# Expert feed-forward on 71 token tiles: first matmul with its weights as the loaded operand, second in high and low parts

## The chip, the cores and the metric

The kernel runs on one core of a Trainium2 chip, in one launch. TensorE (PE, with its weight loads shown as PEld), VectorE (DVE), ScalarE (ACT), GpSimd (POOL) and the DMA queues of SyncE and GpSimd run side by side and wait for each other on semaphores. The metric is the device time of one execution in microseconds.

## The reference

`x` is 16 sequences of 256 rows with 512 columns (4096 rows), and the program applies four blocks to it, each as `x = x + tanh(gate) * block(layernorm(x))`. The change is in the last, a mixture of 8 experts with the best 2 for each row:

```python
router_logits = x_flat @ w_router
top_vals, top_idx = jax.lax.top_k(router_logits, TOP_K)          # 2 of 8
probs = jax.nn.softmax(top_vals, axis=-1)
w_tok = jnp.zeros((N, E)).at[rows, top_idx].add(probs)
h = jnp.einsum('nc,ecd->ned', x_flat, w_fc)                      # 512 -> 512
h = jnp.square(jax.nn.relu(h))
y = jnp.einsum('ned,edc->nec', h, w_proj)                        # 512 -> 512
out = jnp.einsum('nec,ne->nc', y, w_tok)
```

The blocks before it (a long convolution mixed with per-head products, a gated sum over 32 small experts, a cross attention with 8 heads) are the same in both kernels.

## The kernel before

After attention the kernel computes the router's logits, picks two experts for each row, counts, and lays the 8192 (row, expert) picks out in tiles of 128 picks that all belong to one expert: `TILES9` = 71 tiles. `slots` holds for each tile the row number of each of its 128 picks, `share` the weight of each, and `TEi` for each tile the offset of its expert in the weights. `WF` and `WP` keep all eight experts' first and second weights in SBUF, 8 x 2048 float32 per partition each.

The stage for the experts, from about 1187 us to the end, works tile by tile:

- `gather(j)` (POOL): an indirect DMA brings the 128 normed rows of the tile from DRAM into `xs[j % 3]`.
- `across(j)` (PE, L1511): four float32 transposes turn the rows into `pX`; `columns(j)` (DVE, L1823) copies them to `xc[j % 2]`.
- `up(j)` (PE, L1519): four float32 matmuls, with 128 columns of `xc` as the loaded operand and 512 columns of the expert's `WF` moving. A float32 matmul shows as two records, so eight records. The result has picks on the partitions.
- ReLU (ACT, L1654) into `hr`; `back(j)` (PE, L1526): four float32 transposes; the square (ACT, L1657) into `hT`.
- `down(j)` (PE, L1534): four float32 matmuls, `hT` loaded, `WP` moving, into `pY`.
- scaling by `share` (DVE, L1832) into `ys[j % 2]`, and a scatter (POOL, L1336), an indirect DMA that adds the rows to the output in DRAM. Each scatter waits until the one before has landed (`s_add9`).

Each engine has its instructions in the order in which they are written, and waits where a semaphore asks it to. `after(signal, eng, n)` waits only for n above 0; the buffers of this stage are double, and a producer waits by it for the consumer of two tiles ago. PE's order is `up(j + 1)`, `across(j + 2)`, `down(j)`, `back(j + 1)` for each j. The small buffers of this stage lie in `XN`, which until then held the rows of x.

## Time and profile before

| | us |
|---|---|
| median of 3 runs | 1759.55 (1759.21 to 1763.59) |
| the profiled execution | 1759.9 |
| its span, first to last instruction | 1758.2 |
| PE busy | 1593.6 (91%) |
| DVE busy | 931.6 (53%) |
| ACT busy | 710.3 (40%) |
| POOL busy | 960.2 (55%) |

Busy time is read per engine, and an average over stages with different limits says little of one stage; in the views that follow the stage of the experts is cut out. A merged row of a timeline stands for several instructions ("x8"), with the start of the first and the time to the end of the last. Matmuls are pipelined, so the spacing of their starts, not the duration of one, is what a run of them costs. "L1519" is line 1519 of the kernel.

### The profile page before, as it was taken

The numbers are of one execution on the slowest core, as the hardware profiler recorded it, in microseconds if no ns is written. First come the engines' busy times: TensorE is split into PE (matmuls) and PEld (weight loads), VectorE is DVE, ScalarE is ACT, GpSimd is POOL, SyncE is SP. The second block draws the span as 40 slices with busy tenths as digits, with TensorE's granted clock in tenths as the row PEclk, the third lists the DMA queues.
The fourth block names the chain that finished last, engine by engine and source line by source line (L and its number), as shares of the span: only waits on it lengthen the run. The fifth ranks groups of instructions, "written<-read, shape, count | busy, mean of one in ns | idle before, by whom it ended". The sixth has DMA issues, their size and how long they took to land.

```text
span 1758.2 us, 24233 instructions
## 1 busy us (share of the span) xinstructions
PE 1593.6 (91%) x6970; PEld 881.5 (50%) x6970; DVE 931.6 (53%) x1555; ACT 710.3 (40%) x1367; POOL 960.2 (55%) x978
## 2 busy tenths in 40 slices
PE   5999999987584499999999999868999999999997
PEld 4677777765251244444444443564444444444443
DVE  7788888887365467777777774361111111111111
ACT  6332333226327167777777777531111111111111
POOL 4788888864027367888888888202333333333332
PEclk9999999988697589999999999969999999999999
DMA  6344434438358945666666661832334334334333
GB/s 237 126 131 140 138 131 131 135 114 216 61 174 287 240 109 140 163 162 162 156 157 151 155 157 38 293 138 60 64 69 72 65 68 72 65 67 72 66 66 48
DMA packets 110375, 224.00 MB, mean 127 GB/s; under 512 B 12257, under 2 KB 12257, under 8 KB 109409
## 3 DMA queue, kind: packets, MB, share of 16 engines
q1 hardware_dynamic: 94400, 185.88, 37.0%
q0 software_dynamic: 15904, 37.23, 12.1%
q8 instruction: 38, 0.62, 0.1%
q14 instruction: 33, 0.26, 0.1%
HBM read 146.71 MB, written 75.84 MB: 127 GB/s over the span
## 4 chain that ended last, share of the span: by engine, by line
PE 62%; DVE 1%; ACT 1%; DMA 1%; issue 0%; SPq 0%; POOL 0%; DVEq 0%; ACTq 0%; POOLq 0%
PE pA L1519 14%; PE pO L1534 14%; PE pB L1370 9%; PE pO L1380 7%; PE pA L1352 7%; PE pO L1393 4%; PE pA L1511 2%; PE pB L1526 2%; PE pO L1503 1%; PE pB L1361 1%; PE pA L1442 1%; PE pA L1449 1%; DVE low L1668 0%; PE pB L1468 0%; DMA qs<-q_low 0%
## 5 line engine op out<-in xcount | busy, mean ns | idle before, releaser
L1668 DVE TENSOR_REDUCE low<-pA 128x2 f32<-128x1024 f32 x256 | 307.7, 1223 | 145.9 <-PE pA L1352 134.8
L1599 ACT ACTIVATE pt<-pB 128x512 f32<-128x512 f32 x512 | 287.1, 593 | 128.6 <-PE pB L1370 123.2
L424 PE MATMUL y<-kv,toep 128*128 128x288 f32 x1280 | 327.8, 413 | 9.0 <-DVEq L63 5.8
L1336 POOL DMA_INDIRECT out_rows<-XN,slots x71 | 112.6, 1587 | 357.5 <-DVE XN L1832 353.4
L424 PEld LDWEIGHTS y<-kv,toep 128*128 128x128 f32 x1280 | 239.0, 191 | 97.5 <-DVEq L63 34.0
L1519 PE MATMUL pA<-WF,XN 128*128 x568 | 257.8, 597 | 1.1 <-DVE XN L1823 0.9
L1534 PE MATMUL pO<-WP,XN 128*128 x568 | 255.6, 593 | 0.8 <-ACT XN L1657 0.8
L1370 PE MATMUL pB<-qs,ks 98*128 98x512 f32 x512 | 229.3, 452 | 2.7 <-ACT pt L1599 2.4
L1352 PE MATMUL pA<-ks,qs 96*128 96x512 f32 x512 | 190.7, 418 | 34.4 <-DMA qs<-q_low 33.0
L1370 PEld LDWEIGHTS pB<-qs,ks 98*128 98x128 f32 x512 | 97.0, 191 | 192.5 <-ACT pt L1599 150.2
L1823 DVE COPY XN<-pA 128x512 f32<-128x512 f32 x71 | 49.1, 691 | 258.3 <-PE pA L1511 258.3
L1304 POOL TENSOR_TENSOR part_sum<-pt 128x1024 f32<-128x1024 f32 x64 | 152.1, 2377 | 20.3 <-ACT pt L1599 12.9
L1832 DVE TENSOR_SCALAR XN<-pO,share 128x512 f32<-128x512 f32 x71 | 53.3, 751 | 200.2 <-PE pO L1534 200.2
L1309 POOL TENSOR_TENSOR part_sum<-part_sum,pt 128x1024 f32<-128x1024 f32 x64 | 152.4, 2381 | 7.0 <-POOL part_sum L1304 3.8
L1519 PEld LDWEIGHTS pA<-WF,XN 128*128 128x128 f32 x568 | 103.2, 192 | 104.8 <-issue 104.8
L1534 PEld LDWEIGHTS pO<-WP,XN 128*128 128x128 f32 x568 | 102.5, 190 | 103.3 <-issue 103.3
L1657 ACT ACTIVATE XN<-pB 128x512 f32<-128x512 f32 x71 | 42.4, 597 | 260.2 <-PE pB L1526 260.2
L394 ACT ACTIVATE ym<-y 128x384 f32<-128x384 f32 (+1 forms) x128 | 52.5, 410 | 230.7 <-PE y L424 230.7
L1380 PE MATMUL pO<-pt,vt 128*32 128x512 f32 x1024 | 136.6, 607 | 0.0
L1352 PEld LDWEIGHTS pA<-ks,qs 96*128 96x128 f32 x512 | 100.9, 200 | 61.0 <-DMA qs<-q_low 34.5
L1654 ACT ACTIVATE XN<-pA 128x512 f32<-128x512 f32 x71 | 42.4, 597 | 216.0 <-PE pA L1519 216.0
L362 POOL TENSOR_TENSOR R<-ym,qc 128x384 f32<-128x384 f32 (+1 forms) x128 | 99.2, 795 | 55.8 <-ACT ym L394 54.7
(252 smaller groups left out, 2006.8 us busy)
## 6 DMA issues: line engine op xcount, KB each, us to landing
ks<-ctx_high SPq DMA_DIRECT2D x64, 256.0 KB, 4.7
qs<-q_high SPq DMA_DIRECT2D x64, 256.0 KB, 6.3
kc<-in_ctx_conv SPq DMA_DIRECT2D x32, 384.0 KB, 5.4
XN<-in_x SPq DMA_DIRECT2D x16, 512.0 KB, 10.0
toep<-kernel_and_skip SPq DMA_DIRECT2D x32, 256.0 KB, 3.5
ct<-in_ctx SPq DMA_DIRECT2D x16, 512.0 KB, 6.4
ctx_high<-kh SPq DMA_DIRECT2D x16, 512.0 KB, 4.4
ctx_low<-kl SPq DMA_DIRECT2D x16, 512.0 KB, 5.1
```

The source lines that it names most:

```text
L362: pool.tensor_tensor(ap(R[half], n0 * 4 * HD0 + 1, [[4 * HD0, n], [HD0 + 1, D4 - 1], [1, HD0]]), ap(ym[half], n0 * MID, [[MID, n], [HD0, D ...
L424: m = pe.matmul(y[half].rearrange("p (l n) c -> p l n c", l=CB)[:, l, :, 0:PAIRS], toep[u][:, (l - s) * P:(l - s + 1) * P], kv[u][:, half, ...
L1304: pool.tensor_tensor(part_sum[:, 2 * n:2 * n + 2], pt[0][:, 2 * n:2 * n + 2], pt[1][:, 2 * n:2 * n + 2], ALU.add).then_inc(s_add, 1)
L1309: pool.tensor_tensor(part_sum[:, 2 * n:2 * n + 2], part_sum[:, 2 * n:2 * n + 2], pt[2][:, 2 * n:2 * n + 2], ALU.add).then_inc(s_add, 1)
L1336: pool.indirect_dma_start(out=out["out"], out_offset=bass.IndirectOffsetOnAxis(ap=slots[:, j:j + 1], axis=0), in_=ys[j % 2], in_offset=Non ...
L1352: m = pe.matmul(pA[n % 2][:, half, :], qs[u][0:NS, h, m0:m0 + P].bitcast(F32R), ks[u][0:NS, h, :].bitcast(F32R), start=True, stop=True)
L1370: pe.matmul(bank(u, n), ks[u][0:NS + 2, h, s * P:(s + 1) * P].bitcast(F32R), qs[u][0:NS + 2, h, :].bitcast(F32R), start=True, stop=True).t ...
L1380: m = pe.matmul(pO[u % 2][h * HD1:(h + 1) * HD1, :], vt[u][:, s, h * HD1:(h + 1) * HD1], pt[s][:, h, :], start=(s == 0), stop=(s == CB - 1))
L1519: m = pe.matmul(pH[j % 2], xc[j % 2][:, k, :], ap(WF, e + k * C, [[1, C]]), start=(k == 0), stop=(k == CB - 1))
L1534: m = pe.matmul(pY[j % 2], hT[j % 2][:, k, :], ap(WP, e + k * C, [[1, C]]), start=(k == 0), stop=(k == CB - 1))
L1599: act.activation(pt[s][:, h, :], bank(u, n), ACT.Exp, scale=SCALE1).then_inc(s_exp, 1)
L1668: dve.tensor_reduce(ap(low[u % 2], t % CB * NH + t // CB, [[NH, 2], [1, 1]]), pA[n % 2], op=ALU.max, axis=AX.X, negate=True).then_inc(s_re ...
```

## The change

The first matmul's operands trade places: the expert's weights are loaded, 128 x 128 at a time, and the tile's 128 columns move. So `pH` holds the hidden values with the hidden dimension on the partitions (block b in columns 128b to 128b + 127), and `back` is not needed. ACT copies the tile's expert weights out of `WF` into `fc[j % 2]` first (`fc_at`), 2048 float32 per partition.

The second matmul is done in float32r, as three products: high part of the hidden values by high part of the weights, high by low, and low by high. ACT makes the weights' high part by a copy that rounds to float32r (`proj_high`), DVE the low part as the difference (`proj_low`, one buffer only). For the hidden values ACT takes the ReLU into `hq` (`picks_above`), DVE multiplies it with max(pH, 0) to have the square (`squares`), ACT rounds it to `hh` (`picks_high`), and DVE takes the difference into `hl` (`picks_low`). The new buffers lie where `XN` lies.

```diff
--- before.py
+++ after.py
@@ -97,6 +97,11 @@
     s_eps = sem("s_eps")
     s_gates = sem("s_gates")
 
+    with ExitStack() as rows:
+        sb(rows, "tiles", [P, 8 * C])
+        hh, hl = ([sb(rows, f"{n}{i}", [P, C]) for i in range(2)] for n in ("hh", "hl"))
+        fc, wph = ([sb(rows, f"{n}{i}", [P, CB * C]) for i in range(2)] for n in ("fc", "proj_high"))
+        wpl = sb(rows, "proj_low", [P, CB * C])
     XN = sb(whole, "XN", [P, UNITS, ROW])
 
     def x_rows(b):
@@ -1087,14 +1092,13 @@
             sem(n + "_7", st) for n in ("s_t", "s_ev", "s_l", "s_lg", "s_m", "s_gap", "s_e2", "s_took", "s_pos",
                                         "s_in", "s_R", "s_w", "s_dve", "s_cnt", "s_Q", "s_V", "s_W", "s_pl", "s_wz", "s_slots")]
 
-        xc, hr, hT, ys = ([ap(XN, (3 + 2 * n + i) * C, [[1, C]]) for i in range(2)] for n in range(4))
-        xc, hT = ([t.rearrange("p (k n) -> p k n", n=P) for t in ring] for ring in (xc, hT))
+        xc, ys = ([ap(XN, (3 + 2 * n + i) * C, [[1, C]]) for i in range(2)] for n in range(2))
+        hq = ap(XN, 7 * C, [[1, C]])
         pX, pH = ([bank[:, i] for i in range(2)] for bank in pA)
         pX = [bank.rearrange("p (k n) -> p k n", n=P) for bank in pX]
-        pG = [bank.rearrange("p (k n) -> p k n", n=P) for bank in pB]
         pY = pO
-        s_xt, s_xc, s_h, s_hr, s_g, s_hT, s_y, s_ys, s_add9 = [sem(n + "_9", st) for n in (
-            "s_xt", "s_xc", "s_h", "s_hr", "s_g", "s_hT", "s_y", "s_ys", "s_add")]
+        s_xt, s_xc, s_h, s_hr, s_hq, s_low, s_w9, s_y, s_ys, s_add9 = [sem(n + "_9", st) for n in (
+            "s_xt", "s_xc", "s_h", "s_hr", "s_hq", "s_low", "s_w", "s_y", "s_ys", "s_add")]
 
         def after(signal, eng, n):
 
@@ -1512,43 +1516,35 @@
                 t.then_inc(s_xt, 1)
 
             def up(j):
-                e = pe.value_load(TEi[0:1, j:j + 1], min_val=0, max_val=(E1 - 1) * CB * C)
+                pe.wait_ge(s_w9, 2 * j + 1)
                 pe.wait_ge(s_xc, j + 1)
-                after(s_hr, pe, j - 1)
-                for k in range(CB):
-                    m = pe.matmul(pH[j % 2], xc[j % 2][:, k, :], ap(WF, e + k * C, [[1, C]]), start=(k == 0), stop=(k == CB - 1))
+                after(s_hq, pe, j - 1)
+                for b in range(CB):
+                    for k in range(CB):
+                        m = pe.matmul(pH[j % 2][:, b * P:(b + 1) * P], fc[j % 2][:, k * C + b * P:k * C + b * P + P], xc[j % 2][:, k * P:(k + 1) * P],
+                                      start=(k == 0), stop=(k == CB - 1))
                 m.then_inc(s_h, 1)
 
-            def back(j):
-                pe.wait_ge(s_hr, j + 1)
-                after(s_hT, pe, j - 1)
-                for k in range(CB):
-                    t = pe.transpose(pG[j % 2][:, k, :], hr[j % 2][:, k * P:(k + 1) * P], ident)
-                t.then_inc(s_g, 1)
-
             def down(j):
-                e = pe.value_load(TEi[0:1, j:j + 1], min_val=0, max_val=(E1 - 1) * CB * C)
-                pe.wait_ge(s_hT, j + 1)
+                pe.wait_ge(s_low, 2 * j + 2)
                 after(s_ys, pe, j - 1)
                 for k in range(CB):
-                    m = pe.matmul(pY[j % 2], hT[j % 2][:, k, :], ap(WP, e + k * C, [[1, C]]), start=(k == 0), stop=(k == CB - 1))
+                    rows = slice(k * P, (k + 1) * P)
+                    weights = slice(k * C, (k + 1) * C)
+                    for n, (picks, proj) in enumerate(((hh, wph[j % 2]), (hh, wpl), (hl, wph[j % 2]))):
+                        m = pe.matmul(pY[j % 2], picks[j % 2][:, rows].bitcast(F32R), proj[:, weights].bitcast(F32R),
+                                      start=(k == 0 and n == 0), stop=(k == CB - 1 and n == 2))
                 m.then_inc(s_y, 1)
 
             across(0)
-            pe.wait_ge(s_wf, 16 * E1)
             up(0)
             across(1)
-            back(0)
-            pe.wait_ge(s_wp, 16 * E1)
-            pe.wait_ge(s_slots, 2)
             for j in range(TILES9):
                 if j + 1 < TILES9:
                     up(j + 1)
                 if j + 2 < TILES9:
                     across(j + 2)
                 down(j)
-                if j + 1 < TILES9:
-                    back(j + 1)
...
@@ -1648,13 +1644,42 @@
                                        scale=ap(weight, c * G + n, [[1, 1]]))
                 m.then_inc(s_W, 1)
 
+            def fc_at(j):
+                e = act.value_load(TEi[0:1, j:j + 1], min_val=0, max_val=(E1 - 1) * CB * C)
+                after(s_h, act, j - 1)
+                act.activation(fc[j % 2], ap(WF, e, [[1, CB * C]]), ACT.Copy).then_inc(s_w9, 1)
+
+            def proj_high(j):
+                e = act.value_load(TEi[0:1, j:j + 1], min_val=0, max_val=(E1 - 1) * CB * C)
+                after(s_y, act, j - 1)
+                act.activation(wph[j % 2].bitcast(F32R), ap(WP, e, [[1, CB * C]]), ACT.Copy).then_inc(s_w9, 1)
+
+            def picks_above(j):
+                act.wait_ge(s_h, j + 1)
+                after(s_low, act, 2 * j - 1)
+                act.activation(hq, pH[j % 2], ACT.Relu).then_inc(s_hr, 1)
+
+            def picks_high(j):
+                act.wait_ge(s_hq, j + 1)
+                after(s_y, act, j - 1)
+                act.activation(hh[j % 2].bitcast(F32R), hq, ACT.Copy).then_inc(s_hr, 1)
+
+            act.wait_ge(s_slots, 1)
+            act.wait_ge(s_wf, 16 * E1)
+            fc_at(0)
+            act.wait_ge(s_wp, 16 * E1)
+            proj_high(0)
+            fc_at(1)
+            picks_above(0)
+            picks_high(0)
             for j in range(TILES9):
-                act.wait_ge(s_h, j + 1)
-                after(s_g, act, j - 1)
-                act.activation(hr[j % 2], pH[j % 2], ACT.Relu).then_inc(s_hr, 1)
-                act.wait_ge(s_g, j + 1)
-                after(s_y, act, j - 1)
-                act.activation(hT[j % 2], pG[j % 2], ACT.Square).then_inc(s_hT, 1)
+                if j + 1 < TILES9:
+                    proj_high(j + 1)
+                if j + 2 < TILES9:
+                    fc_at(j + 2)
+                if j + 1 < TILES9:
+                    picks_above(j + 1)
+                    picks_high(j + 1)
 
         @block.vector
         def _(dve):
@@ -1820,16 +1845,43 @@
             def columns(j):
                 dve.wait_ge(s_xt, j + 1)
                 after(s_h, dve, j - 1)
-                dve.tensor_copy(xc[j % 2], pX[j % 2]).then_inc(s_xc, 1)
-
-            columns(0)
-            columns(1)
-            for j in range(TILES9):
-                if j + 2 < TILES9:
-                    columns(j + 2)
+                dve.tensor_copy(xc[j % 2], pX[j % 2].rearrange("p k n -> p (k n)")).then_inc(s_xc, 1)
+
+            def proj_low(j):
+                e = dve.value_load(TEi[0:1, j:j + 1], min_val=0, max_val=(E1 - 1) * CB * C)
+                dve.wait_ge(s_w9, 2 * j + 2)
+                after(s_y, dve, j)
+                dve.tensor_tensor(wpl.bitcast(F32R), ap(WP, e, [[1, CB * C]]), wph[j % 2], ALU.subtract).then_inc(s_low, 1)
+
+            def squares(j):
+                dve.wait_ge(s_h, j + 1)
+                dve.wait_ge(s_hr, 2 * j + 1)
+                dve.scalar_tensor_tensor(hq, pH[j % 2], 0.0, hq, ALU.max, ALU.mult).then_inc(s_hq, 1)
+
+            def picks_low(j):
+                dve.wait_ge(s_hr, 2 * j + 2)
+                dve.tensor_tensor(hl[j % 2].bitcast(F32R), hq, hh[j % 2], ALU.subtract).then_inc(s_low, 1)
+
+            def scaled(j):
                 dve.wait_ge(s_y, j + 1)
                 after(s_add9, dve, 16 * (j - 1))
                 dve.tensor_scalar(ys[j % 2], pY[j % 2], share[:, j:j + 1], None, ALU.mult).then_inc(s_ys, 1)
+
+            columns(0)
+            columns(1)
+            squares(0)
+            picks_low(0)
+            for j in range(TILES9):
+                if j > 0:
+                    scaled(j - 1)
+                proj_low(j)
+                if j + 1 < TILES9:
+                    squares(j + 1)
+                if j + 2 < TILES9:
+                    columns(j + 2)
+                if j + 1 < TILES9:
+                    picks_low(j + 1)
+            scaled(TILES9 - 1)
 
 
 # ---- launch: one core; numpy lays the inputs out, and takes the output's rows apart again ----
```

On PE the place is the middle of the stage, one tile. Names: `pA` holds `pX` and `pH`, `pB` is `pG`, `pO` is `pY`, `XN` are the small buffers, `s_x90` the landing of a gather. Before:

```order
L1519 MATMUL pA<-WF,XN 128x512
L1511 MATMUL pA<-ident,XN 128x128 [waits s_xc_9,s_x90]
L1511 MATMUL pA<-ident,XN 128x128 x3
L1530 TENSOR_LOAD TEi
L1530 ISA x2
L1534 ISA [waits s_ys_9,s_hT_9]
L1534 MATMUL pO<-WP,XN 128x512
```

and with the change:

```order
L1524 MATMUL pA<-XN,fc 128x128 [waits s_hq_9,s_xc_9,s_w_9]
L1524 MATMUL pA<-XN,fc 128x128 x15
L1515 MATMUL pA<-ident,XN 128x128 [waits s_xc_9,s_x90]
L1515 MATMUL pA<-ident,XN 128x128 x3
L1535 MATMUL pO<-proj_high,hh 128x512 [waits s_ys_9,s_low_9]
L1535 MATMUL pO<-proj_low,hh 128x512
L1535 MATMUL pO<-proj_high,hl 128x512
```

`across` keeps its place between `up` and `down`; the transposes of L1526 are gone, the loads of the expert's offset too, and `down` now waits for the low parts.

On DVE, one tile in the same place. Before:

```order
L1832 TENSOR_SCALAR XN<-pO,share 128x512 [waits s_add_9,s_y_9]
L1823 COPY XN<-pA 128x512 [waits s_h_9,s_xt_9]
L1832 TENSOR_SCALAR XN<-pO,share 128x512 [waits s_add_9,s_y_9]
L1823 COPY XN<-pA 128x512 [waits s_h_9,s_xt_9]
L1832 TENSOR_SCALAR XN<-pO,share 128x512 [waits s_add_9,s_y_9]
```

and with the change:

```order
L1868 TENSOR_SCALAR XN<-pO,share 128x512 [waits s_add_9,s_y_9]
L1851 TENSOR_LOAD TEi
L1851 ISA x2
L1854 ISA [waits s_y_9,s_w_9]
L1854 TENSOR_TENSOR proj_low<-WP,proj_high 128x2048
L1859 SCALAR_TENSOR_TENSOR XN<-pA,XN 128x512 [waits s_hr_9,s_h_9]
L1848 COPY XN<-pA 128x512 [waits s_h_9,s_xt_9]
L1863 TENSOR_TENSOR hl<-XN,hh 128x512 [waits s_hr_9]
L1868 TENSOR_SCALAR XN<-pO,share 128x512 [waits s_add_9,s_y_9]
```

The scaling (L1868) now has `proj_low` right behind it, and `squares`, `columns` and `picks_low` stand between that and the next scaling.

On ACT, one tile. Before there are only the ReLU (L1654) and the square (L1657):

```order
L1654 ACTIVATE XN<-pA 128x512 [waits s_g_9,s_h_9]
L1657 ACTIVATE XN<-pB 128x512 [waits s_y_9,s_g_9]
L1654 ACTIVATE XN<-pA 128x512 [waits s_g_9,s_h_9]
L1657 ACTIVATE XN<-pB 128x512 [waits s_y_9,s_g_9]
L1654 ACTIVATE XN<-pA 128x512 [waits s_g_9,s_h_9]
```

and with the change:

```order
L1653 TENSOR_LOAD TEi
L1653 ISA x2
L1655 ISA [waits s_y_9]
L1655 ACTIVATE proj_high<-WP 128x2048
L1648 TENSOR_LOAD TEi
L1648 ISA x2
L1650 ISA [waits s_h_9]
L1650 ACTIVATE fc<-WF 128x2048
L1660 ACTIVATE XN<-pA 128x512 [waits s_low_9,s_h_9]
L1665 ACTIVATE hh<-XN 128x512 [waits s_y_9,s_hq_9]
```

The two long copies stand ahead of the ReLU of the next tile.

## Rows read from the trace of the kernel before

**Rows 1.** The page: busy us by engine; the chain that ended last, by line.

```profile
PE 1593.6 (91%) x6970; PEld 881.5 (50%) x6970; DVE 931.6 (53%) x1555; ACT 710.3 (40%) x1367; POOL 960.2 (55%) x978
...
PE pA L1519 14%; PE pO L1534 14%; PE pB L1370 9%; PE pO L1380 7%; PE pA L1352 7%; PE pO L1393 4%; PE pA L1511 2%; PE pB L1526 2%; PE pO L1503 1%; PE pB L1361 1%; PE pA L1442 1%; PE pA L1449 1%; DVE low L1668 0%; PE pB L1468 0%; DMA qs<-q_low 0%
```

**Rows 2.** Chain of waits in order of time: start us, us, engine, line.

```profile
1193.14 5.77 PE pA L1519 x8
...
1204.59 3.44 PE pO L1534 x8
1208.47 3.44 PE pA L1519 x8
...
1735.12 3.44 PE pA L1519 x8
...
1743.06 4.84 DMA out_rows<-XN,slots
1748.67 1.55 POOL out_rows L1336
```

**Rows 3.** Busy us of PE, PEld, DVE, ACT, POOL; granted clock; 1200 to 1740.

```profile
1200.00:1740.00 540.00, 539.78 (x1671) 266.02 (x1669) 99.57 (x139) 83.58 (x140) 175.73 (x136) 1.00 0.38 67
```

**Rows 4.** Timeline of one tile: start us, us, engine, line, op.

```profile
1351.58 3.60 PE L1534 MATMUL pO<-WP,XN 128*128 x8
...
1355.02 0.60 PE L1526 MATMUL pB<-ident,XN 128*128 128x128 f32 x4
...
1355.22 0.75 DVE L1832 TENSOR_SCALAR XN<-pO,share 128x512 f32<-128x512 f32 x1 [2.75 <-PE pO L1534]
...
1355.46 3.60 PE L1519 MATMUL pA<-WF,XN 128*128 x8
...
1356.25 1.59 POOL L1336 DMA_INDIRECT out_rows<-XN,slots  x1 [4.87 <-DVE XN L1832]
```

**Rows 5.** Timeline of PE at full clock, float32 with short moving operands.

```profile
487.80 2.40 PE L785 MATMUL pk<-RB,WV 128*128 128x64 f32 x20
...
1181.83 4.29 PE L1503 MATMUL pO<-XN 128*128 128x142 f32 x34
```

**Rows 6.** Timeline of PE in attention; L1352 and L1370 are float32r.

```profile
701.78 0.39 PE L1352 MATMUL pA<-ks,qs 96*128 96x512 f32 x1
...
702.71 0.42 PE L1370 MATMUL pB<-qs,ks 98*128 98x512 f32 x1
...
704.05 0.50 PE L1370 MATMUL pB<-qs,ks 98*128 98x512 f32 x1
...
704.86 0.39 PE L1352 MATMUL pA<-ks,qs 96*128 96x512 f32 x1
...
705.18 1.07 PE L1380 MATMUL pO<-pt,vt 128*32 128x512 f32 x8
```

**Rows 7.** Groups by line and form (mean ns); L1515, ns min/median/max.

```profile
L968 ACT ACTIVATE WV<-WV 128x1024 fp32r<-128x1024 f32 x16 | 16.9, 1057 | 0.5
...
L913 ACT ACTIVATE room<-WV 128x512 f32<-128x512 f32 x16 | 10.0, 626 | 0.0
L1750 DVE TENSOR_TENSOR XN<-numbers,inside 128x1024 f32<-128x1024 f32 x8 | 9.8, 1221 | 0.4
...
L1772 DVE TENSOR_TENSOR XN<-numbers,tile 128x568 f32<-128x568 f32 x8 | 6.0, 744 | 0.4 <-PE pO L1503 0.3
...
L1515 PEldq TENSOR_LOAD <-TEi x71: 296/301/490, 1191.2 to 1731.5; - x71
```

**Rows 8.** Timelines in which DVE starts while POOL works.

```profile
27.87 1.89 POOL L145 TENSOR_TENSOR kv<-kc 128x1024 f32<-128x1024 f32 x1 [2.42 <-DMA kc<-in_ctx_conv]
27.96 1.83 DVE L222 SCALAR_TENSOR_TENSOR work_<-mv,rstd_ 128x8 f32<-128x8 f32 x1
...
1097.01 4.82 POOL L1309 TENSOR_TENSOR part_sum<-part_sum,pt 128x1024 f32<-128x1024 f32 x2
...
1097.78 1.72 DVE L1782 CAST numbers<-numi 128x161 f32<-128x161 int32 x1
```

## The prediction

> **What bounds the kernel now.** I read the page first: TensorE is busy 91% of the span, and two lines of the expert stage, L1519 and L1534, make 28% of the chain that ended last [rows 1]. Then the chain in order of time [rows 2]: from 1204.59 us to the end of the matmuls it is L1534, L1519, L1534, L1519 without a break, eight records in 3.44 us each, and a pair comes every 7.745 us (1208.47 to 1735.12 is 68 pairs). Then the busy times between 1200 and 1740 us [rows 3]: PE 539.78 of 540 us at full granted clock (1.00, that is 2.4 GHz), DVE 99.57, ACT 83.58, POOL 175.73. So the change is worth what it does to PE's sum per tile, as long as the other three keep up.
>
> The timeline of one tile [rows 4] gives that sum as differences of starts. L1534 at 1351.58 to L1526 at 1355.02 is 3.44 us for eight records, 0.430 each; L1526 at 1355.02 to L1519 at 1355.46 is four transposes, 0.109 each. 16 x 0.430 + 8 x 0.109 = 7.75, the measured 7.745. A merged row outlasts its spacings by the last record's overhang: 3.60 - 3.44 = 0.16.
>
> **PE, part by part.**
> - `up` was 3.44 us. Now it is 16 float32 matmuls, thus 32 records of 128 columns, each with its own weight load. Nearest rows at full clock [rows 5], overhang taken off: L1503, 142 columns and new weights for each record, (4.29 - 0.16)/34 = 0.121, what 142 columns take in proportion to L1519; L785, only 64 columns, (2.40 - 0.16)/20 = 0.112, so there the loads set the pace. The transposes, 128 columns, show 0.109. I take 0.112, 3.58 us; bounds 0.109 (3.49) and 0.121 (3.87).
> - `across` stays, 0.44. `back` goes, -0.44.
> - `down` was 3.44. Now it is 12 float32r records of 512 columns. In attention [rows 6] four such start between 701.78 and 702.71 (three spacings and the merged one counted: 0.93 us for four), 0.233 each: 2.80 us. The other end is half of L1519's 0.430, 0.215: 2.58.
> - Switches between float32 and float32r come twice per tile, new in this stage. The L1370 that follows float32 at 704.05 lasts 0.50 in place of 0.39, +0.11. Leaving, L1352 at 704.86 to L1380 at 705.18 is 0.32 in place of 0.233, +0.09 [rows 6]. Bounds 0 and 0.30 per tile (both, and half as much again); I take 0.15, since PE's look ahead may hide one of them behind `across`.
>
> Sum: 3.58 + 0.44 + 2.80 + 0.15 = 6.97 us in place of 7.745, so -0.775 per tile.
>
> The Trainium skill, "TensorE: Matmul & The Clock Gate", section "Part 3: Packing small matmuls", says that a weight load overlaps matmuls in flight only where their row groups differ; here all use all rows, so by that rule each record would pay its load and its stream in turn. The trace disagrees: L1503 and L1519 run at 0.121 and 0.430 with a full-row load for each record. It is rival 3.
>
> **What must hide beside it.** Durations for 2048 elements are drawn on from two sizes [rows 7]. ACT, SBUF to SBUF: 512 in 0.626, 1024 in 1.057, so 2048 in 1.92 us. DVE with two SBUF inputs: 568 in 0.744, 1024 in 1.221, so 2048 in 2.29 us.
> - ACT per tile: two copies 3.84, ReLU 0.60, float32r copy 0.63: 5.07 us, where it was 83.58 over 69.7 tiles, 1.2. Fits in 6.97.
> - DVE: `columns` 0.69, `scaled` 0.75 [rows 4], `proj_low` 2.29, `squares` 0.75 (as `scaled`, one PSUM input of 512), `picks_low` 0.69: 5.17 us, where it was 1.4. Fits.
> - The expert's number is read from SBUF twice on ACT and once on DVE. On PE that read takes 0.30 us [rows 7] of the sequencer, with two register steps perhaps 0.5, while the engine works. On ACT it comes behind a copy of 0.63 or 1.92, on DVE behind `scaled`: hidden, charged nothing; exposed it is 0.5 on DVE, and 1.0 on ACT.
> - The single `proj_low` buffer is the tightest wait. DVE may write it when `down(j-1)` is over, and `down(j)` waits for it; behind `down(j)` on PE stand `up(j+2)` and all else. Between them PE has `up(j+1)` and `across(j+2)`, 4.02 us. DVE has the handover 0.2 (overhang 0.16 and 0.04: 1355.18 to 1355.22), `scaled` 0.75 and `proj_low` 2.29: 3.24. Cover left: 0.8 us.
> - The long ring spans two tiles: from the end of `down(j-1)` on, `proj_high(j+1)` 1.92, `fc_at(j+2)` 1.92, ReLU 0.60, `squares` 0.75, `columns` 0.69, `picks_low` 0.69, `scaled` 0.75, `proj_low` 2.29, `down(j+1)` 2.80: 12.41, with handovers 13.0, against 13.94. Cover left: 0.9 us per two tiles.
> - POOL's program is the same. Its loop: a scatter lands 4.84 us after its start, and the next starts 0.77 after that (1743.06 + 4.84 = 1747.90, 1748.67) [rows 2]: 5.61 us per tile, under 6.97.
>
> **Start and end.** `up(0)` waits for the same `columns(0)` as now, 1193.14, in a slow stretch (5.77 us for eight records, 3.44 later); `fc_at(0)`, ready with the slots before the first gather, is done by then. `down(0)` waits for `up(0)` (1198.9), `across(1)` and `columns(1)` (1200.1), `squares`, the copy, `picks_low` and `proj_low`: 1204.5, where it is 1204.59 now. The last `down(70)` waits for `scaled` and `proj_low` after `down(69)`, 3.2 us where `back` and the square now take 1.4; it is 0.6 shorter itself, and some of the rest runs beside the scatter chain behind it. Together +0.5 us.
>
> **The sum.** 69 spacings x -0.775 = -53.5, and +0.5: -53. The profiled execution took 1759.9 us (span 1758.2), the median of the three runs is 1759.55. 1759.9 - 53 = 1706.9; against the median it would be 1706.5. I say 1706. This case's own ends: best 3.49 + 0.44 + 2.58 = 6.51, -85, 1675; worst 3.87 + 0.44 + 2.80 + 0.30 = 7.41, -23, 1737.
>
> **Rivals.**
> 1. *The ring through ACT and DVE decides.* For it: ACT goes from 1.2 to 5.1 us per tile and DVE from 1.4 to 5.2, in a ring with 0.9 us of cover per two tiles; exposed reads of the expert's number would use that up. Against: each sum alone fits, and handovers are 0.04. With 2.0 us more the ring is 15.0, 7.5 per tile: 69 x -0.245 = -17, 1743.
> 2. *The port that DVE and POOL share; it ends slower.* DVE's cast of 161 elements takes 1.72 us [rows 8]: it starts inside the first of two POOL additions (1097.01, 2.4 each) and ends at 1099.50, just as that one ends. Another DVE operation, on 8 elements with two SBUF inputs, starts at 27.96 and ends at 29.79, POOL's ends at 29.76. So one holds the other off for a whole instruction. `proj_low` lasts 2.29 us, has two SBUF inputs, and starts right behind `scaled`, which is what wakes the scatter 0.28 later (1355.97, 1356.25 in [rows 4]). If each scatter is held 2.29, its loop is 5.61 + 2.29 = 7.90: 71 x +0.155 = +11, 1771. It decides from a hold of 1.36 per tile (6.97) and loses from 2.13 (7.745). The other way round, `proj_low` held for the scatter's 1.59, makes 3.24 + 1.59 - 4.02 = +0.81, 7.78 per tile, 1762. Against: a scatter that starts late in its tile meets only the rest of `proj_low`, so the hold shrinks before it binds, and DVE starts first by 0.3 us.
> The Trainium skill, "SBUF — State Buffer", section "SBUF: two separate sides", calls the pair an exclusive lock, which a DVE operation with two SBUF inputs takes only against a GpSimd one that reads SBUF. The two rows agree. Whether an indirect DMA's issue is held too, no row shows.
> 3. *Weight loads exposed in `up`.* The loads' pace 0.112 plus half of 0.215 for 128 columns is 0.219, `up` 7.0 us, the tile 10.4: +183, 1943. L1503 speaks against it.
>
> **How the numbers follow.** The forecast has 0.75, rival 1 0.10, rival 2 0.09 (0.07 by the scatter's loop, 0.02 by a held DVE), rival 3 0.02; 0.04 is left for what I don't see. The range 1680 to 1745 cuts the forecast's fast tail, where all bounds fall well at once, and takes in rival 1. What a measurement can tell from no change is 0.3%, about 5 us. Faster by more: 0.75 + 0.10 + 0.01 = 0.86; within: 0.04; slower: 0.10.
>
> **What would show it.** Right: in the stage's chain, 32 records of `up` 0.112 apart, 12 of `down` 0.233 apart with the first some 0.1 longer, pairs every 6.9 to 7.0 us, PE still busy nearly throughout. Wrong: PE idle before `down` with `proj_low` as releaser (its cover is gone), before `up` with `fc` or the columns (rival 1); `scaled` waiting for a landed scatter, or a scatter longer than 1.59 (rival 2); `up` near 0.2 apart (rival 3). My number fails if float32r takes more than 0.233 with 128 rows of weights, or a switch more than 0.15.

## The result, and the profile after

The changed kernel takes 1698.9 us (median of 4 runs, 1694.96 to 1701.35), beside 1759.99 for the kernel before on the same chip (1759.21 to 1763.59): a ratio of 0.9647, interval 0.962 to 0.9673. The forecast was 1706 with a range of 1680 to 1745. The profiled execution took 1696.54 us, its span is 1694.8.

First the page: busy time by engine, then the head of the chain that ended last, by line. They answer to [rows 1].

```profile
PE 1525.5 (90%) x8674; PEld 1054.9 (62%) x8674; DVE 1185.5 (70%) x1768; ACT 969.3 (57%) x1509; POOL 1043.7 (62%) x978
...
DMA out_rows<-XN,slots 22%; PE pB L1374 10%; PE pO L1384 8%; PE pA L1356 7%; PE pO L1397 4%; PE pO L1535 1%; PE pO L1507 1%; PE pA L1524 1%; DMA XN<-normed_rows,slots 1%; PE pB L1365 1%; PE pA L1446 1%; PE pA L1453 1%; DVE low L1693 1%; PE pB L1472 0%; POOL out_rows L1340 0%
```

TensorE is 68 us less busy, DVE 254 and ACT 259 us more. The chain hardly names `up` and `down` any more (L1524 and L1535, 1% each); it names the scatters. That is a trap, and the next view shows it: the busy times of PE, PEld, DVE, ACT and POOL and the granted clock, in the stage's steady part (as [rows 3]) and while the last `down` runs.

```profile
1200.00:1670.00 470.00, 466.94 (x3291) 429.79 (x3290) 345.26 (x345) 331.38 (x276) 254.69 (x135) 1.00 0.43 77
...
1679.00:1684.00 5.00, 5.00 (x12) 3.80 (x12) 0.00 (x0) 0.00 (x0) 1.38 (x1) 0.50 0.41 52
```

PE is still busy 99.3% of the steady part, so PE's sum per tile is still what a tile costs. The chain goes through the scatters because each of them starts 0.81 us after the one before has landed (median of tiles 5 to 65), and the walk back never leaves that loop. What is new is 3 us of idle PE in the first row and a clock of 0.50 in the second.

The timeline of one tile (start us, us, engine, line, operation; rows between are left out at "..."), which answers to [rows 4]:

```profile
1402.60 3.77 PEld L1524 LDWEIGHTS pA<-XN,fc 128*128 128x128 f32 x32
...
1402.82 3.73 PE L1524 MATMUL pA<-XN,fc 128*128 128x128 f32 x32
...
1403.02 0.75 DVE L1868 TENSOR_SCALAR XN<-pO,share 128x512 f32<-128x512 f32 x1 [0.31 <-PE pO L1535]
...
1403.83 2.29 DVE L1854 TENSOR_TENSOR proj_low<-WP,proj_high 128x2048 fp32r<-128x2048 f32 x1
...
1404.94 2.64 POOL L1340 DMA_INDIRECT out_rows<-XN,slots  x1 [2.84 <-DMA out_rows<-XN,slots]
...
1406.39 0.60 PE L1515 MATMUL pA<-ident,XN 128*128 128x128 f32 x4
...
1406.74 0.48 PE L1535 MATMUL pO<-proj_high,hh 128*128 128x512 f32 x1
...
1407.06 0.40 PE L1535 MATMUL pO<-proj_low,hh 128*128 128x512 f32 x1
...
1407.30 0.40 PE L1535 MATMUL pO<-proj_high,hl 128*128 128x512 f32 x1
```

L1524 is `up`: 1402.82 to 1406.39 is 3.57 us for 32 records, 0.1115 each. L1535 is `down`. Its first record shows 0.35 after `across` started, before four transposes of 0.109 can be through, and the second comes 0.32 later to make up for it; after that the records stand 0.24 and 0.23 apart. From the end of `across`'s four spacings (1406.39 + 0.44 = 1406.83) to the next `up` at 1409.60 it is 2.77 us. The usual spacing from `up` to `up` is 3.57 + 0.435 + 2.77 = 6.77 us, where it was 7.745.

The groups by line and form (busy us, mean ns, then idle before and its releaser) show the two things that were new to me: the scatters' issue takes 2.74 us where it took 1.59 [rows 4], and PE waits at `across` for a gather. Of those waits 5.0 us stood in the kernel before too, ahead of its first tiles, as the last row shows; the other 2.8 are new.

```profile
L1340 POOL DMA_INDIRECT out_rows<-XN,slots x71 | 194.7, 2742 | 215.4 <-DMA out_rows<-XN,slots 181.0 <-DVE XN L1868 34.4
...
L1515 PE MATMUL pA<-ident,XN 128*128 128x128 f32 x284 | 43.7, 277 | 7.8 <-DMA XN<-normed_rows,slots 7.7
```

```profile
L1511 PE MATMUL pA<-ident,XN 128*128 128x128 f32 x284 | 43.1, 275 | 5.0 <-DMA XN<-normed_rows,slots 5.0
```

### The profile page after: what moved, and what is told of

Read it like the earlier page. It is cut to its first block, busy times and chain, and to the rows that moved or that the text cites. A ratio compares the mean times of both kernels' runs of the same rounds, so it can differ in the third digit from the quotient of the medians.

```text
span 1694.8 us, 27929 instructions
## 1 busy us (share of the span) xinstructions
PE 1525.5 (90%) x8674; PEld 1054.9 (62%) x8674; DVE 1185.5 (70%) x1768; ACT 969.3 (57%) x1509; POOL 1043.7 (62%) x978
## 4 chain that ended last, share of the span: by engine, by line
PE 35%; DMA 23%; issue 3%; DVE 2%; ACT 1%; POOL 0%; SPq 0%; POOLq 0%; DVEq 0%; ACTq 0%
DMA out_rows<-XN,slots 22%; PE pB L1374 10%; PE pO L1384 8%; PE pA L1356 7%; PE pO L1397 4%; PE pO L1535 1%; PE pO L1507 1%; PE pA L1524 1%; DMA XN<-normed_rows,slots 1%; PE pB L1365 1%; PE pA L1446 1%; PE pA L1453 1%; DVE low L1693 1%; PE pB L1472 0%; POOL out_rows L1340 0%
## 5 line engine op out<-in xcount | busy, mean ns | idle before, releaser
L1340 POOL DMA_INDIRECT out_rows<-XN,slots x71 | 194.7, 2742 | 215.4 <-DMA out_rows<-XN,slots 181.0
L1524 PEld LDWEIGHTS pA<-XN,fc 128*128 128x128 f32 x2272 | 266.1, 193 | 7.7 <-ACT fc L1650 1.2
L1524 PE MATMUL pA<-XN,fc 128*128 128x128 f32 x2272 | 266.8, 276 | 1.7 <-DVE XN L1848 1.7
L1655 ACT ACTIVATE proj_high<-WP 128x2048 fp32r x71 | 135.8, 1912 | 81.1 <-PE pO L1535 81.1
L1854 DVE TENSOR_TENSOR proj_low<-WP,proj_high 128x2048 fp32r<-128x2048 f32 x71 | 162.8, 2293 | 5.6 <-issue 1.6
L1650 ACT ACTIVATE fc<-WF 128x2048 f32 x71 | 134.5, 1894 | 4.7 <-DVEq L1843 4.7
L150 POOL TENSOR_TENSOR kv<-kc 128x1024 f32<-128x1024 f32 x64 | 121.1, 1892 | 5.0 <-PEq L418 3.1
L1029 POOL DMA_INDIRECT XN<-normed_rows,slots x71 | 70.5, 993 | 83.1 <-DVEq L1843 60.8
L1535 PE MATMUL pO<-proj_high,hh 128*128 128x512 f32 x284 | 117.8, 415 | 3.5 <-DVE proj_low L1854 3.5
```

What stands on the lines that cost most here:

```text
L1340: pool.indirect_dma_start(out=out["out"], out_offset=bass.IndirectOffsetOnAxis(ap=slots[:, j:j + 1], axis=0), in_=ys[j % 2], in_offset=Non ...
L1524: m = pe.matmul(pH[j % 2][:, b * P:(b + 1) * P], fc[j % 2][:, k * C + b * P:k * C + b * P + P], xc[j % 2][:, k * P:(k + 1) * P], start=(k ...
L1655: act.activation(wph[j % 2].bitcast(F32R), ap(WP, e, [[1, CB * C]]), ACT.Copy).then_inc(s_w9, 1)
L1854: dve.tensor_tensor(wpl.bitcast(F32R), ap(WP, e, [[1, CB * C]]), wph[j % 2], ALU.subtract).then_inc(s_low, 1)
```

## The experiments

`e1` to `e4` ran on one chip, `e5` to `e8` on another, `e9` to `e11` on a third, each group beside the kernel before, whose median there was 1760.08, 1757.45 and 1758.21 us; so across groups it is the ratios to it that compare. Every edit is shown against the changed kernel, with lines left out at "...". "Spacing" is the median time from one `up` to the next; "excess" is what the 68 spacings from tile 2 to tile 70 take beyond 68 such medians; the tail is from the start of `up(70)` to the end of the span. All three are read from the one profiled execution of each kernel. Before: spacing 7.745, excess 0, tail 23.2. After: 6.773, 4.8, 25.5.

### The two halves of the change alone

`e1`: `up` is turned, its weights are copied by ACT, the squares go straight to `down`, and `down` stays float32 from `WP`.

```diff
-                    for n, (picks, proj) in enumerate(((hh, wph[j % 2]), (hh, wpl), (hl, wph[j % 2]))):
-                        m = pe.matmul(pY[j % 2], picks[j % 2][:, rows].bitcast(F32R), proj[:, weights].bitcast(F32R), ...
+                    m = pe.matmul(pY[j % 2], hh[j % 2][:, k * P:(k + 1) * P], ap(WP, e + k * C, [[1, C]]), ...
```

> One half of the change alone: the first matmul has its weights loaded and 128 columns moving, the second stays in float32 (eight records from WP, no parts of the weights, no low part of the picks; the square goes straight into the buffer that is loaded). Theory, PE's sum decides: up 3.57 (32 x 0.1115), across 0.44, down 3.44, no back: 7.45 us per tile against 7.745, so 69 x -0.295 = -20 us, about 1739. PE idle nowhere, scatter's issue 1.59 us again, since no DVE operation with two SBUF inputs is left. Rival, that turning costs what back saved (weight loads exposed, fc copies late): about 1760.

`e2`: `up` and `back` as before, `down` by parts.

```diff
-                        m = pe.matmul(pH[j % 2][:, b * P:(b + 1) * P], fc[j % 2][:, ...], xc[j % 2][:, ...], ...
...
+                    m = pe.matmul(pH[j % 2], xc[j % 2][:, k * P:(k + 1) * P], ap(WF, e + k * C, [[1, C]]), ...
...
+            def back(j):
...
+                    t = pe.transpose(pG[j % 2][:, k, :], hr[j % 2][:, k * P:(k + 1) * P], ident)
```

> The other half alone: the first matmul and back as before, the second matmul by parts in float32r (12 records), with proj_high and proj_low made per tile. Theory, PE's sum: up 3.44, across 0.44, back 0.44, down 2.76: 7.08 us per tile, 69 x -0.665 = -46 us, about 1713; with the first half's -20 the two add to the whole change's -61 plus what its end and its late gathers cost (some 5). The scatter is held by proj_low here too (2.3 to 2.9 us in place of 1.59). Rival, switches between float32 and float32r cost 0.15 and more per tile: 7.23, about 1724.

Measured: `e1` 1739.64 us (1735.97 to 1742.19), ratio 0.9893 (0.9877 to 0.9908), spacing 7.443. `e2` 1718.15 us (1717.07 to 1720.85), ratio 0.9768 (0.9753 to 0.9783), spacing 7.080. From their chains of waits, `e1` and then `e2`:

```profile
1249.51 3.57 PE pA L1524 x32
1253.52 3.44 PE pO L1533 x8
1256.96 3.57 PE pA L1524 x32
```

```profile
1254.96 2.77 PE pO L1542 x12
1258.17 3.44 PE pA L1525 x8
1262.04 2.77 PE pO L1542 x12
```

Turning `up` is worth 0.302 us per tile (it costs 0.13 more than the old `up` and saves `back`), the parts 0.665. Together 0.967, and the change has 0.972: the halves add, and neither pays for the other. In `e1` no float32r stands in the stage, in `e2` and in the changed kernel it does, and `down` is 2.77 in both. In whole times `e1` met what was expected of it, and `e2` took 5 us more than its 1713: its spacing is the expected 7.08, but its tail is 26.4 us, 3.2 longer than before, and in its trace the stage begins 1.1 us later.

### What holds the scatter's issue

In the tile above the scatter starts 1.1 us into `proj_low`. That ends at 1406.12, and the scatter's record at 1404.94 + 2.64 = 1407.58, 1.46 behind it, near the whole of its old 1.59. Four kernels ask whether `proj_low` causes it, and what it costs.

`e3` puts `proj_low` ahead of `scaled`, so that nothing of it stands where the scatter is issued:

```diff
             for j in range(TILES9):
+                proj_low(j)
                 if j > 0:
                     scaled(j - 1)
-                proj_low(j)
```

> The changed kernel with one thing moved: on DVE proj_low(j) goes ahead of the scaling of tile j-1, so that the scatter wakes when proj_low is over. Theory, the scatter's issue (2.74 us in place of 1.59) is held by proj_low, the DVE operation with two SBUF inputs, until that ends: the issue is back at 1.59 us, the gathers behind it come 1 us earlier, the late across of some tiles (gaps of 0.4 to 0.8 us, 4 to 5 us in all) are gone. 1692 to 1696. Spacing 6.77 as before. Rival, the shorter tile alone makes the issue long (more DMA traffic, other engines busier): the issue stays at 2.7 us and the time at 1699.

`e4` makes the low part for the first tile alone; for all others DVE reduces 8 elements, and PE reads the first tile's low part (this leaves the low parts of the other weights out of the result):

```diff
-                dve.tensor_tensor(wpl.bitcast(F32R), ap(WP, e, [[1, CB * C]]), wph[j % 2], ALU.subtract).then_inc(s_low, 1)
+                if j == 0:
+                    dve.tensor_tensor(wpl.bitcast(F32R), ap(WP, e, [[1, CB * C]]), wph[j % 2], ALU.subtract).then_inc(s_low, 1)
+                else:
+                    dve.tensor_reduce(fold[:, 0:1], ap(WP, e, [[1, 8]]), op=ALU.max, axis=AX.X).then_inc(s_low, 1)
```

> proj_low is made for the first tile only; for the others DVE does a tiny reduction of 8 elements in its place, so the low parts of the other tiles' weights are left out of the result. PE's work is the same. Theory of the hold: the issue is at 1.59 us; PE stays at 6.77 per tile; gaps gone; and the last down follows the one before within 0.5 us in place of 3.2, so that PE's clock doesn't fall there (2.7 us): about 1689 to 1692. Rival, the issue's length has another cause: 2.7 us stays.

`e7` is `e4` with the reduction over all 2048 weights, so DVE is as long at work as in `proj_low` but has one SBUF input (the same is left out):

```diff
...
+                else:
+                    dve.tensor_reduce(fold[:, 0:1], ap(WP, e, [[1, CB * C]]), op=ALU.max, axis=AX.X).then_inc(s_low, 1)
```

> proj_low's subtraction is made for the first tile only; for the others DVE does in its place a reduction over the same 2048 elements of the weights into one column, which has one SBUF input and about the same length (1024 elements from PSUM take 1.22 us, so some 2.2 us). The low parts of the other tiles' weights are left out of the result. Theory, the scatter's issue is held by a DVE operation with two SBUF inputs: it is 1.59 us here, and the time is the changed kernel's less its gaps, 1693 to 1696. Rival, any long DVE operation behind the scaling holds it: 2.7 us and 1699.

`e8` makes `proj_low` by four subtractions of 512 columns:

```diff
-                dve.tensor_tensor(wpl.bitcast(F32R), ap(WP, e, [[1, CB * C]]), wph[j % 2], ALU.subtract).then_inc(s_low, 1)
+                for q in range(4):
+                    t = dve.tensor_tensor(wpl[:, q * C:(q + 1) * C].bitcast(F32R), ap(WP, e + q * C, [[1, C]]), wph[j % 2][:, q * C:(q + 1) * C], ALU.subtract)
+                t.then_inc(s_low, 1)
```

> proj_low as four subtractions of 512 elements in a row (0.69 us each, about 2.5 us together) in place of one of 2048. Theory, the port is held for one instruction, and given up between two: the scatter gets in at the next boundary, so its issue is held 0.3 us in the mean and at most 0.6, 1.7 to 2.2 us long; the gathers come 0.7 us earlier and most gaps of across go: 3 to 4 us less than the changed kernel. Rival, the sequence holds it as a whole: 2.7 to 3.0 us long and no gain.

Measured: `e3` 1704.23 us (1698.74 to 1706.87), ratio 0.9678 (0.966 to 0.9695); `e4` 1690.1 (1688.56 to 1690.62), 0.9605 (0.959 to 0.962); `e7` 1692.25 (1690.24 to 1693.18), 0.9626 (0.9603 to 0.9648); `e8` 1692.79 (1692.05 to 1697.36), 0.963 (0.9608 to 0.9651). The scatter's group in `e3`, `e4`, `e7` and `e8`, one fence each; for `e7` and `e8` DVE's own group between 1210 and 1670 us stands below it:

```profile
L1340 POOL DMA_INDIRECT out_rows<-XN,slots x71 | 112.7, 1587 | 304.0 <-DVE XN L1868 299.9 <-DMA out_rows<-XN,slots 4.1
...
L1515 PE MATMUL pA<-ident,XN 128*128 128x128 f32 x284 | 44.3, 279 | 12.0 <-DMA XN<-normed_rows,slots 11.6
```

```profile
L1340 POOL DMA_INDIRECT out_rows<-XN,slots x71 | 112.6, 1587 | 289.8 <-DVE XN L1871 285.9 <-DMA out_rows<-XN,slots 3.8
```

```profile
L1340 POOL DMA_INDIRECT out_rows<-XN,slots x71 | 112.7, 1587 | 292.3 <-DVE XN L1871 292.3
...
L1857 DVE TENSOR_REDUCE fold<-WP 128x1 f32 x68 | 155.5, 2286 | 5.0 <-issue 1.3
```

```profile
L1340 POOL DMA_INDIRECT out_rows<-XN,slots x71 | 136.4, 1921 | 269.1 <-DVE XN L1870 269.1
...
L1855 DVE TENSOR_TENSOR proj_low<-WP,proj_high 128x512 fp32r<-128x512 f32 x272 | 169.9, 687 | 5.6 <-issue 1.3
```

Set these beside the changed kernel, and there are four forms of DVE's work and the length of the same POOL instruction with each: 2742 ns with one 2.29-us operation on two SBUF inputs, 1921 with four of 0.69, 1587 (as before) with a reduction of the same 2.29 us that has one SBUF input, and 1587 with next to nothing. So the hold is shown: a running DVE operation with two SBUF inputs keeps the scatter's issue waiting for its own end, and one instruction later the scatter gets through.

The single instructions say the same. In the changed kernel 70 of the 71 scatters start inside `proj_low`; their issues last 1.91 to 3.70 us, and all of them end 1.43 to 1.52 us after `proj_low` does. That leaves some 0.13 of the 1.59 ahead of the held point, and in `e8` three scatters that start 0.13 to 0.15 us ahead of the first quarter are not held (1.59). `e7`'s reduction also writes far less than `proj_low`, so a rival is that DVE's long write holds the scatter; `e10`, further down, speaks against it. There 51 scatters meet `proj_low` at that point and end 1.46 to 1.52 us behind it, while seven that meet `squares` (one input in PSUM, one in SBUF, 512 elements written to SBUF) and six that meet `columns` (PSUM to SBUF) take 1.57 to 1.59 and end earlier than that. Gathers are held in the same way: four in `e10` meet `proj_low`, take 2.55 to 3.00 us in place of 0.99, and end 0.86 us behind it. Whether it is the read of the slots or the writing of descriptors that is held, no run tells.

`e3` was expected to gain and is the slowest of the four. Its ratio can't be told from the changed kernel's (0.9647, 0.962 to 0.9673), but its excess can: 11.0 us against 4.8. The issue is back at 1.59, but `scaled` comes 2.6 us later in the tile (medians over tiles 5 to 65, here and in what follows), and with it the scatter; the gather stands behind the scatter on POOL. It is issued 4.85 us before `across` needs it, where the changed kernel had 5.27, `e8` 6.87, `e4` and `e7` 7.22. A gather lands 4.3 us after its issue at the median and 6.3 at most, so `e3` has 20 late tiles of 68, the changed kernel 10, `e8` one that is hardly late, and `e4` and `e7` none. So the theory that the hold itself is what costs time falls. What costs is a late gather, however it comes to be late.

### What the hold costs: gathers one tile further ahead

```diff
+            after(s_xt, pool, 1)
+            gather(pool, 3)
             for j in range(TILES9):
-                if j + 3 < TILES9:
-                    after(s_xt, pool, j + 1)
-                    gather(pool, j + 3)
+                if j + 4 < TILES9:
+                    after(s_xt, pool, j + 2)
+                    gather(pool, j + 4)
                 pool.wait_ge(s_ys, j + 1)
```

> The changed kernel with POOL's gathers one tile further ahead in its order: gather(j+4) ahead of scatter(j) in place of gather(j+3); across(j+1), which it waits for, is over by then. proj_low and the hold of the scatter stay. Theory, formed from the run with proj_low moved (its issue was 1.59 us again and it was still slower): what costs time is not the hold itself but the gather that stands behind the scatter on POOL; it lands just before across needs it, or after. So here: issue still 2.7 us, across never waits, spacing 6.77 throughout, 4 to 5 us less than the changed kernel beside it. Rival, the late tiles come from the scaling that waits for a landed scatter: gaps before down and across remain and the time is the same.

`e6` is the changed kernel once more, beside it:

> The changed kernel itself once more, to have its time on the chip and in the rounds of the three beside it. Expected 1695 to 1702.

Measured: `e5` 1691.16 us (1688.57 to 1694.41), ratio 0.9616 (0.9596 to 0.9635); `e6` 1696.9 (1694.52 to 1700.99), 0.9656 (0.9634 to 0.9679). The groups of `e5` (its lines are 2 further on):

```profile
L1342 POOL DMA_INDIRECT out_rows<-XN,slots x71 | 186.7, 2629 | 212.6 <-DMA out_rows<-XN,slots 191.9 <-DVE XN L1870 12.6 <-issue 8.1
...
L1517 PE MATMUL pA<-ident,XN 128*128 128x128 f32 x284 | 43.1, 275 | 5.0 <-DMA XN<-normed_rows,slots 5.0
```

The issue is still held, 2.63 us, yet the spacing stays at 6.773 throughout (excess 0.02; the 5.0 us left before L1517 lie before tile 2), since the gathers are issued 12.05 us before they are needed. `e4`, `e7` and `e8`, in which the scatter is held less or not at all, have the same 6.77 and an excess of 0.02 to 0.05 without touching the gathers. So two cures of one illness agree, and the illness is worth 5 us: 5.7 by the medians of `e5` and `e6`, 5.3 by their excess. In the changed kernel a late tile reads like this:

```profile
1376.83 2.81 POOL L1340 DMA_INDIRECT out_rows<-XN,slots  x1 [2.66 <-DMA out_rows<-XN,slots]
...
1379.95 0.99 POOL L1029 DMA_INDIRECT XN<-normed_rows,slots  x1 [0.30 <-issue]
...
1386.04 0.66 PE L1515 MATMUL pA<-ident,XN 128*128 128x128 f32 x4 [0.66 <-DMA XN<-normed_rows,slots]
...
1390.51 3.54 POOL L1340 DMA_INDIRECT out_rows<-XN,slots  x1 [2.79 <-DVE XN L1868]
```

The scatter's issue ends at 1379.64, the gather is issued at 1379.95 and lands 6.05 later (1386.00, by the chain), and `across` starts at 1386.04 after 0.66 of idle PE. Two things meet here: this gather takes 1.75 us longer to land than the median, and it is issued late. Behind an unheld scatter it would have been issued 1.2 earlier (2.81 - 1.59), and the 0.66 would not be there. In most tiles the gather lands in time (in `e6` with 1.0 us to spare at the median); 10 of the 68 have such a gap, 8 in `e6`. Why some gathers take longer to land stays open.

### The tail, and all of it together

`e9` has the gathers of `e5`, the quarters of `e8`, and 14 small matmuls, whose result nobody reads, between the last two `down`. `e11` is `e5` again, beside it.

```diff
+                if j + 1 == TILES9:
+                    for n in range(14):
+                        pe.matmul(pX[1][:, n % CB, :], fc[0][:, n * P:(n + 1) * P], xc[0][:, 0:P], start=True, stop=True)
                 down(j)
```

> The version that the runs point to: the changed kernel, the gathers one tile further ahead, proj_low in four pieces, and 14 turned matmuls without use (28 records, 3.1 us, into a free PSUM bank) ahead of the last down, where PE otherwise idles 3.6 us and its granted clock falls to 0.5 (the last 12 records took 4.6 to 5.5 us in place of 2.75). Theory: spacing 6.77, scatter's issue 1.9, and the last down at full clock, 1.9 us less, of which the scatter chain behind leaves 1.5: 1689.5 where the kernel with the gathers alone has 1691. Rival, the clock falls all the same: 1691.

> The kernel with the gathers one tile further ahead once more, beside the version with all three edits, since they differ by less than a chip from another. Expected 1689 to 1693.

The chains' ends (start us, us, engine, line), of the changed kernel and of `e9`:

```profile
1673.08 2.75 PE pO L1535 x12
1676.66 2.30 DVE proj_low L1854
1679.01 5.50 PE pO L1535 x12
1685.56 1.55 POOL out_rows L1340
```

```profile
1670.21 2.86 PE pO L1537 x12
1674.52 1.90 DVE proj_low L1860 x3
1676.46 3.07 PE pO L1537 x12
1680.59 1.55 POOL out_rows L1342
```

In the changed kernel PE idles from 1675.83 to 1679.01, and the last 12 records then run at a granted clock of 0.50: 5.50 us to the end of the last one, where `down(69)` takes 2.98. With something to do in between they take 3.07 at full clock, and the tail is 23.4 us against `e11`'s 24.7. But `e6`, the same kernel as the changed one, shows that the clock does not always fall. Its last `down` also comes after 3.19 us of idle PE, and its granted clock stays at 1.00 (the second row is a stretch, with busy times as above):

```profile
1680.52 0.50 PE L1535 MATMUL pO<-proj_high,hh 128*128 128x512 f32 x1 [3.19 <-DVE proj_low L1854]
...
1680.50:1683.50 3.00, 2.98 (x12) 2.17 (x12) 0.00 (x0) 0.00 (x0) 1.39 (x1) 1.00 0.39 40
```

Eight traces have 12 records behind 3.1 to 3.4 us of idle PE: they take 5.5 us in two (the changed kernel, `e2`), 4.6 in five (`e3`, `e5`, `e7`, `e8`, `e11`) and 3.04 in `e6`. So the one trace of `e9` agrees with the filler keeping the clock up, and doesn't show it. In the total it can't be told: `e9` 1691.62 (1691.58 to 1696.53), ratio 0.963 (0.9613 to 0.9647); `e11` 1693.2 (1685.7 to 1697.59), 0.9627 (0.9602 to 0.9652). The best version I can name is thus the changed kernel with its gathers one tile further ahead; the filler and the quarters add nothing that can be measured.

### How near the next bound is

`e10` is `e5` without the first of the three products, which leaves the high by high part out of the result. PE then has 5.85 us per tile (6.773 less four records of 0.2305), and what keeps the tile longer must be the ring of copies or the scatters' loop.

```diff
-                    for n, (picks, proj) in enumerate(((hh, wph[j % 2]), (hh, wpl), (hl, wph[j % 2]))):
+                    for n, (picks, proj) in enumerate(((hh, wpl), (hl, wph[j % 2]))):
...
-                                      start=(k == 0 and n == 0), stop=(k == CB - 1 and n == 2))
+                                      start=(k == 0 and n == 0), stop=(k == CB - 1 and n == 1))
```

> The changed kernel with the gathers one tile further ahead, and the second matmul with two of its three products (high by high is left out of the result), so that PE's sum per tile is 3.57 + 0.44 + 1.84 = 5.85 us. It tells where the next limit stands. Theory, a scatter's hold only reaches to the end of proj_low, so its loop is 5.6 us whatever the hold, and the ring through ACT and DVE is (12.41 - 0.92 - 0.16 for the measured, shorter ACT and DVE rows + 0.6)/2 = 5.96 at most: 5.85 to 6.0 per tile, 1628 to 1638. Rival, the loop is 5.61 plus the hold of 1.1 seen at 6.77: 6.7 per tile, 1687.

Measured: 1638.95 us (1633.8 to 1643.47), ratio 0.9322 (0.9297 to 0.9347), 5.96 us per tile; the time is a little above the range expected, the tile within it. Two rows of its timeline, one tile apart, and a scatter between them:

```profile
1401.34 3.81 PE L1526 MATMUL pA<-XN,fc 128*128 128x128 f32 x32
...
1404.46 2.34 POOL L1342 DMA_INDIRECT out_rows<-XN,slots  x1 [2.65 <-DMA out_rows<-XN,slots]
...
1407.35 3.74 PE L1526 MATMUL pA<-XN,fc 128*128 128x128 f32 x32
```

Its waits between 1300 and 1550 us (who waits, for whom, us, times, longest):

```profile
POOL out_rows L1342 <- DMA out_rows<-XN,slots: 106.9, 39, 2.9
...
ACT hh L1667 <- DVE XN L1861: 34.3, 41, 1.2
DVE XN L1861 <- ACT XN L1662: 32.1, 42, 1.1
...
ACT proj_high L1657 <- PE pO L1537: 12.9, 41, 0.7
```

The loop of the scatters does not add its whole hold: that would have been 5.61 + 2.29 = 7.9, or at least the 6.7 of the other theory, and 5.96 was measured. At this pace the mean issue shrinks to 1.84 us. What is left over PE's 5.85 is 0.11 us per tile. ACT and DVE hand the squares to and fro there, and DVE's `columns`, which stands behind `squares`, now comes last: in 60 of the 63 tiles from 5 to 67 `up` starts 0.10 us after `columns` ends, where the changed kernel had 0.91 at the median. So the ring through ACT and DVE sets the 5.96, as far as one trace shows it. In the changed kernel it has 0.8 us of room. The scatters' loop has none to show there, as each scatter waits for the one before, but it gives way: 4.84 + 0.77 = 5.61 unheld and a mean hold of 1.16 make 6.77, PE's tile, and in `e10` the hold shrinks with the tile.

## Why the prediction was right, and where it was off

**What bounds the kernel: right.** PE's sum sets the tile before and after, and PE is busy 99.3% of the steady part.

**`up`: right.** Predicted 0.112 per record and 3.58 us, measured 0.1115 and 3.57. The Trainium skill, "TensorE: Matmul & The Clock Gate", section "Part 3: Packing small matmuls", says that a load overlaps only where row groups differ; by that every load would be exposed, since all use all row groups. This stage disagrees: the page after lists 2272 loads of 193 ns each for L1524, and the records come 111.5 ns apart. Rival 3 falls.

**`down`: nearly right.** 0.233 per record was taken from attention; here the median over 67 tiles, of the ten spacings behind the second record, is 0.2305, so 2.77 for twelve instead of 2.80.

**The switches: the step of the working that failed.** 0.15 us per tile was read out of single spacings in attention. In this stage (medians over 67 tiles) the first record of `down` starts 0.028 after the transposes' last, the next comes 0.316 later, ten spacings take 2.305, and `up` follows the last record after 0.228. With the last transpose's own 0.109 taken off that is 2.768 us, and twelve even spacings are 2.766: both switches together cost nothing that shows. `e2` has the same 2.77. The bound below, 0, was right, and the value should have been there: 0.09 or 0.11 more on one record says nothing as long as the records around it are not added up. The small terms together make 6.97 - 6.773 = 0.20 us per tile, 13.4 us over 68 tiles, more than the whole distance to the result.

**What must hide beside it: right for the engines.** ACT's copies 1.894 and 1.912 (1.92 predicted), `proj_low` 2.293 (2.29), squares 0.692 (0.75), the records' lengths per tile add up to 5.02 us on ACT and 5.11 on DVE (5.07 and 5.17). `proj_low` ends 0.62 us ahead of `down` at the median, where 0.8 of cover was predicted. The reads of the expert's number cost nothing, as said. Rival 1 did not happen; `e10` shows it waiting some 0.8 us below.

**Rival 2: the mechanism is there, and it does not decide.** The scatter's issue is held, to the end of a DVE operation with two SBUF inputs, by 2.742 - 1.587 = 1.16 us on the mean. That is under the 1.36 from which I had it decide, and it stays there for the reason given against it: a scatter that starts late meets only the rest of `proj_low`, so the loop settles at 5.61 + 1.16 = 6.77, PE's own sum. A scatter longer than 1.59 was on the list of signs of being wrong; it came, and the forecast held, so it was not a sign of that by itself. The Trainium skill, "SBUF — State Buffer", section "SBUF: two separate sides", has the lock for two-input DVE operations against GpSimd's reads; `e7` (one input, no hold) and `e8` (a hold of one short operation) agree with it and show that an indirect DMA's issue counts among what is held. Of the two rows that I had agree with it, only the second has two SBUF inputs; the cast has one, and the sentence as I put it does not cover that row. What I had not seen is the gather that stands behind the scatter on POOL: the working followed the scatter's own loop and not what is queued behind it. With the gathers that are slow to land, this cost 4.8 us.

**Start and end.** From `up(0)` to `up(2)` it is 14.2 us where it was 15.2, nearly the one spacing that the sum had counted there (0.775). The tail is 2.3 us longer, not 0.5. About half of that is the granted clock of 0.50 behind the idle stretch, which I had not counted: in `e6`, where the clock stays up, the tail is 24.3 us, 1.1 longer than before.

**The sum,** for the profiled execution: predicted 1706.9, measured 1696.5, -10.4. Spacing 68 x -0.197 = -13.4; late tiles +4.8; tail +1.8 over the 0.5 allowed; start -0.2; and the expert stage began 3.35 us earlier than in the profiled execution of before, of which 2.6 is a stretch just ahead of it that ran at a granted clock of 0.50 for 20.5 us instead of 27.3. The change does not touch that part, and I don't count it as its gain; in the traces of the other runs that have `up` turned, the stage begins anywhere from 1189.6 to 1195.1 us. Together -10.35.

So the sign and the size come from the two large terms, which the halves confirm one by one (`e1`, `e2`); the small ones were off by 2 to 13 us, with both signs, and that they cancel in part is luck.

## What to carry to other kernels

When one engine is busy 99% of a stage, the stage costs that engine's sum of spacings, and spacings are read between starts at full clock, many at a time: a median over dozens of records tells the price of a switch, one odd record does not. Price a new wait or a held instruction by what is queued behind it on its engine: here the scatter had room, and the gather behind it did not, and issuing the gather one tile earlier gave the 5 us back. A chain of waits that names a DMA for 22% of the span proves nothing as long as the busy engine has no idle time.

## What the runs showed of the hardware that I had not expected

- The issue of an indirect DMA on POOL is held by a DVE operation that has two SBUF inputs until that one ends: 2.74 us with one of 2.29 us, 1.92 with four of 0.69 us, 1.59 with a one-input reduction of 2.29 us. Operations with one SBUF and one PSUM input do not hold it (seven scatters of `e10`, 1.57 to 1.59).
- The hold is decided at the start of the issue: scatters that start 0.13 to 0.15 us ahead of such an operation are through (`e8`), and held ones end 1.46 us after it at the median, however long they waited.
- PE goes from float32 to float32r and back at no measurable cost (0.002 us per tile, over 67 tiles).
- After 3.2 us of idle PE, `down` ran at a granted clock of 0.50 and took 5.50 us; in another execution of the same kernel (`e6`), after as long a gap, it took 3.04 at a granted clock of 1.00. With 14 small matmuls in the gap (`e9`) it took 3.07, also at 1.00, which one execution can't set apart from that.
